# Four chained transformer blocks on one core: the second feed-forward product with its operands swapped

## The reference, cut to what matters

```
ca = _mha(x, enc_output, enc_output, memory_mask, ca_wq, ...)
x  = _ln(x + ca, ln2_g, ln2_b)
ff = relu(x @ ff_w1 + ff_b1) @ ff_w2 + ff_b2      # 128 -> 512 -> 128
x  = _ln(x + ff, ln3_g, ln3_b)
```

## Time and profile before

| | |
|---|---|
| median of 3 runs | 814.97 us (814.9 to 818.01) |
| the profiled execution's own time | 817.6 us |
| its span, first to last instruction | 815.8 us |
| mean granted clock of TensorE, as a share of full speed | 0.944 |
| TensorE busy | 87% |
| VectorE busy | 65% |
| ScalarE busy | 55% |
| GpSimd busy | 37% |

### The profile page before, as it was taken

How to read it: one execution, slowest core, us unless ns; L and a number is a source line. 1 busy time by engine, 2 the same in 40 slices (tenths; PEclk the granted TensorE clock), 3 DMA queues, 4 the chain that set the end, 5 groups by cost and what they waited for, 6 DMA issues and landing times.

```text
span 815.8 us, 26360 instructions
## 1 busy us (share of the span) xinstructions
PE 708.1 (87%) x9248; PEld 471.6 (58%) x9248; DVE 531.0 (65%) x1329; ACT 445.2 (55%) x1242; POOL 304.5 (37%) x497
## 2 busy tenths in 40 slices
PE   2999999999999999999977977777724789999996
PEld 1565666777766666666654755555522456666774
DVE  0698888888888877788872422222222566888784
ACT  1466666766667777777653232222202434676884
POOL 2244444566665333326666100000036663443110
PEclk9999999999999999999986999999975767999998
DMA  8333333223233111111100101111112110111110
GB/s 252 85 79 82 86 81 83 54 60 89 81 91 104 31 28 34 35 27 47 41 22 36 36 26 41 39 42 40 30 39 63 44 39 22 31 30 29 47 42 27
DMA packets 61085, 44.85 MB, mean 55 GB/s; under 512 B 18240, under 2 KB 55488, under 8 KB 59840
## 3 DMA queue, kind: packets, MB, share of 16 engines
q1 hardware_dynamic: 56592, 27.42, 12.0%
q10 hardware_dynamic: 2352, 12.00, 6.0%
q0 software_dynamic: 2048, 4.20, 1.6%
HBM read 22.68 MB, written 14.61 MB: 46 GB/s over the span
## 4 chain that ended last, share of the span: by engine, by line
PE 66%; issue 14%; POOL 7%; DVE 6%; ACT 3%; DMA 1%; ACTq 1%; SPq 0%; POOLq 0%; DVEq 0%
PE ps L560 10%; PE ps L602 9%; PE ps L784 5%; PE ps L722 4%; PE ps L793 4%; PE ps L578 4%; PE ps L655 3%; DVE hid_t L1264 3%; PE ps L730 3%; PE ps L643 3%; PE ps L677 3%; POOL k_by_j L485 2%; PE ps L802 2%; PE ps L587 2%; PE ps L750 2%
## 5 line engine op out<-in xcount | busy, mean ns | idle before, releaser
L1065 DVE TENSOR_REDUCE top<-ps 128x16 f32<-128x1024 f32 (+1 forms) x96 | 108.9, 1134 | 67.7 <-PE ps L560 66.9
L560 PE MATMUL ps<-k_by_j,q_t 32*64 32x256 f32 (+1 forms) x1536 | 126.7, 401 | 0.4 <-issue 0.2
L602 PE MATMUL ps<-cst,prob 128*128 128x128 f32 x704 | 122.3, 295 | 0.8 <-ACT prob L920 0.7
L477 POOL TENSOR_TENSOR rstd<-spread,half_neg 128x1 f32<-128x1 f32 x80 | 44.3, 553 | 207.5 <-DVE spread L1157 119.2
L485 POOL TENSOR_TENSOR k_by_j<-k_t,cst 128x512 f32<-128x512 f32 (+1 forms) x96 | 94.8, 988 | 71.9 <-ACT k_t L901 36.8
L602 PEld LDWEIGHTS ps<-cst,prob 128*128 128x128 f32 x704 | 78.5, 146 | 62.6 <-issue 59.2
L1080 DVE TENSOR_TENSOR prob<-ps,top 128x1024 f32<-128x1024 f32 (+1 forms) x96 | 108.8, 1134 | 0.7
L920 ACT ACTIVATE prob<-prob 128x1024 f32<-128x1024 f32 (+1 forms) x96 | 94.8, 987 | 20.3 <-DVE prob L1080 19.4
L1031 DVE RECIPROCAL inv<-ps 128x128 f32<-128x128 f32 x96 | 91.6, 954 | 11.7 <-PE ps L730 7.8
L518 POOL DMA_INDIRECT got<-expert_out,source x32 | 30.8, 963 | 158.8 <-DMA expert_out<-rows_out 150.2
L1264 DVE COPY hid_t<-ps 128x512 f32<-128x512 f32 x39 | 27.0, 691 | 95.0 <-PE ps L802 95.0
(11 more groups left out here) (160 smaller groups left out, 1287.9 us busy)
## 6 DMA issues: line engine op xcount, KB each, us to landing
sorted_rows<-zero_rows ACTq DMA_DIRECT2D x32, 272.0 KB, 2.7
stage_x<-x_t SPq DMA_DIRECT2D x80, 64.0 KB, 1.8
mow<-in_mow SPq DMA_DIRECT2D x18, 256.0 KB, 3.1
stage_kv<-in_ctx_t SPq DMA_DIRECT2D x64, 64.0 KB
stage_m<-in_m SPq DMA_DIRECT2D x80, 32.0 KB, 1.9
rows_in<-sorted_rows SPq DMA_DIRECT2D x39, 64.0 KB, 1.8
expert_out<-rows_out SPq DMA_DIRECT2D x39, 64.0 KB, 1.5
wat<-in_wat ACTq DMA_DIRECT2D x1, 1280.0 KB, 6.5
```

What stands on the lines that cost most here:

```text
L560: mm = pe.matmul(ps[S * b:S * b + S, 2 * p + bank, r * nj * S:(r + 1) * nj * S].rearrange("p (h k) -> p h k", k=S), q_t[rows_g, p, S * b:S ...
L602: mm = pe.transpose(ps[:, 2 * p + half, k * 128:(k + 1) * 128], prob[:, p, q * 128:(q + 1) * 128], ident)
L1065: dve.tensor_reduce(top[:, p, 0:nh].rearrange("p (b h) -> p b h", b=2), sc, AX.X, ALU.max).then_inc(top_d, 1)
```

## The change

The second product takes `hid_f` as its stationary operand and `ffw2` as the moving one. Its result has tokens in partitions, so VectorE adds `x_tok` to it straight from bank 7. The ScalarE copy (L854), the transpose (L675), the quarter `TURN` and the semaphores `f_o` and `f_turn` go. The bias, now one number per column, is added once, ahead of everything, to the row `b2` that ends up in `x_tok` of phase 1; `x_t`, which feeds the first product, takes its own `b2` from `vec` and stays as it was. The next pair's F waited for `f_o` and now waits for `f_y`, since VectorE is now the one that reads bank 7.

```diff
-ROWS = [..., "bo0", "bo1", "bo4"]
+ROWS = [..., "bo0", "bo1", "bo4", "ffb2"]
...
                 pr = follows(at, OFF_FY, FF)                 # TensorE
                     wait_own(pe, f_r, pr)
                     for c in range(HC):
-                        mm = pe.matmul(ps[:, B_F, 0:TOK], ffw2[:, 0, c, :], hid_f[:, pr.p, c, :], start=c == 0, stop=c == HC - 1)
+                        mm = pe.matmul(ps[:, B_F, 0:D], hid_f[:, pr.p, c, :], ffw2[:, 0, c, :], start=c == 0, stop=c == HC - 1)
                     mm.then_inc(f_acc, 1)
...
                     wait_pair(pe, norm_d, pr)
-                    if pr.phase == FF or pr.phase == FF + 1:
-                        done = follows(at, OFF_FN, FF)
-                        if done is not None:
-                            wait_own(pe, f_y, done)
...
-                    done = follows(at, OFF_FY, FF)
-                    if done is not None:
-                        wait_own(pe, f_o, done)
-                        pe.transpose(ps[:, B_OUT, TURN], sum_f[:, done.p, :], ident).then_inc(f_turn, 1)
-
                     pe.matmul(ps[:, B_OUT, OUT], heads_t[:, pr.p, :], wat[:, pr.phase, 3, :], start=True, stop=True)
...
-                    wait_own(pe, f_o, pr, 1)
+                    wait_own(pe, f_y, pr, 1)                  # ahead of F
                     wait_pair(pe, xt_e, pr)
...
-                pr = follows(at, OFF_FY, FF)                 # ScalarE
-                if pr is not None:
-                    wait_own(act, f_acc, pr)
-                    wait_own(act, f_turn, pr, 2)
-                    act.activation(sum_f[:, pr.p, :], ps[:, B_F, 0:TOK], ACT.Identity, bias=v("ffb2")).then_inc(f_o, 1)
...
+                dve.tensor_tensor(rows[:, ROW["b2"], :], rows[:, ROW["b2"], :], rows[:, ROW["ffb2"], :], ALU.add).then_inc(set_bias, 1)
...
-                    wait_own(dve, f_turn, pr)                # VectorE
+                    wait_own(dve, f_acc, pr)
                     wait_own(dve, f_nn, pr, 2)
                     wait_pair(dve, res_d, pr)
-                    dve.tensor_tensor(y_f[:, p, :], ps[:, B_OUT, TURN], x_tok[:, pr.i, :], ALU.add).then_inc(f_y, 1)
+                    dve.tensor_tensor(y_f[:, p, :], ps[:, B_F, 0:D], x_tok[:, pr.i, :], ALU.add).then_inc(f_y, 1)
```

More of the change, by code:

```diff
@@ L60 @@
 VECS = ["bq0", "bk0", "bq1", "bk1", "bq4", "bk4", "bv0", "bv1", "bv4",
-        "g1", "b1", "g2", "b2", "n1", "n2", "n3", "gL2", "bL2", "ffb2", "l3b1", "l3b2"] + \
+        "g1", "b1", "g2", "b2", "n1", "n2", "n3", "gL2", "bL2", "l3b1", "l3b2"] + \
        [f"ffb1_{c}" for c in range(HC)]
 VCOL = {name: n for n, name in enumerate(VECS)}
-ROWS = ["g1", "b1", "g2", "b2", "g3", "b3", "gL2", "bL2", "bo0", "bo1", "bo4"]
+ROWS = ["g1", "b1", "g2", "b2", "g3", "b3", "gL2", "bL2", "bo0", "bo1", "bo4", "ffb2"]
 ROW = {name: n for n, name in enumerate(ROWS)}
@@ L240, in build @@
         B_PROJ, B_HEADS, B_OUT, B_F = 4, 5, 6, 7
-        XT, FB, OUT, TURN = (slice(128 * n, 128 * n + 128) for n in range(4))
+        XT, FB, OUT = (slice(128 * n, 128 * n + 128) for n in range(3))
         B_SH, B_SY = (0, 1), (2, 3)
@@ L269, in build @@
         kj_d, rstd_d, gsc_d, res_d = (sem(k) for k in ("kj_d", "rstd_d", "gsc_d", "res_d"))
-        f_h, f_r, f_acc, f_o, f_turn, f_y, f_st, f_ag, f_sp, f_rs, f_nn, f_z, f_w, f_x, f_ms, f_rr, f_xn, f_back, f_xt = (
-            sem(f"f_{k}") for k in ("h", "r", "acc", "o", "turn", "y", "st", "ag", "sp", "rs", "nn", "z", "w", "x",
+        f_h, f_r, f_acc, f_y, f_st, f_ag, f_sp, f_rs, f_nn, f_z, f_w, f_x, f_ms, f_rr, f_xn, f_back, f_xt = (
+            sem(f"f_{k}") for k in ("h", "r", "acc", "y", "st", "ag", "sp", "rs", "nn", "z", "w", "x",
                                     "ms", "rr", "xn", "back", "xt"))
@@ L460, in slot @@
                         pool.wait_ge(loaded["rows"], 16)
-                        pool.wait_ge(set_bias, 3)
+                        pool.wait_ge(set_bias, 4)
                     wait_pair(pool, norm_d, pr)
@@ L1021, in residuals @@
                     .then_inc(set_bias, 1)
-                dve.wait_ge(set_bias, 3)
+                dve.wait_ge(set_bias, 4)
             def slot(at):
```

## The result

The changed kernel takes 855.74 us (median of 4 runs, 854.63 to 857.09), the kernel before in the same measurement 815.6 us (814.9 to 818.01). The ratio is 1.0487, with a 95% interval of 1.046 to 1.0515: 40 us slower. The predicted range (834 to 856) holds it by 0.3 us; the predicted 843 is 13 us short. The profiled execution took 857.09 us, with a span of 855.3. Three executions of two kernels of the experiments took far longer than the rest (2729, 3354 and 1020 us), and the ratios leave them out.

What follows compares the result with a forecast made beforehand. TensorE was taken to set the pace, VectorE close behind. F's waits over 15 slots (28.0 us), slot 38's -0.1 and the bias row's 0.3 summed to +28.2, so 815.0 + 28 = 843 us; range 834 to 856.

Steps and rivals of the forecast that it cites:

- F waits for `y_f` of its own slot: F on TensorE overwrites bank 7, so must wait for VectorE's late sum in the same slot; 15 slots, 28.0 us together.
- The size of the wait: Delay of F per slot: 1.77 us fixed, 2.11 in the loop, 1.97 first two, 1.27 last two; 28.0 us.
- so an earlier OUT does not help it: In fixed slots `y` on VectorE follows the subtraction by 0.03 us, so VectorE's side gets no earlier.
- The transpose: One transpose a slot leaves TensorE in 16 slots: 0.13 us each, 2.1 us taken alone, at most 4.8.
- The copy on ScalarE: L854, 0.37 us, 16 times, goes; ScalarE idles ahead of it and then waits for TensorE, so it gives nothing.
- The 0.3 us for the bias row: Adding the bias is one more 128x128 row on VectorE near 32 us, taken in full at 0.3 us.
- PV stays behind F: TensorE products run in program order, so PV can't fill the gap: term 1.77 us, else 0.74 and sum about +12.
- the clock column should stay at 1.00 in this stage: Sign of the main forecast: TensorE keeps its upper clock in the feed-forward stage; 837 to 849 us, chance 0.72.
- the clock falls too: Rival: gaps of 1.6 to 2.0 us in 15 slots cost TensorE its upper clock; +10 to +27 us, chance 0.18.
- absorbed: Rival: TensorE's 0.25 us wait and VectorE's 0.33 us idle vanish in the new rhythm; +19, 834 us, chance 0.06.
- not slower: Rival: `f_y` is there before TensorE reaches F, leaving the transposes' gain; -2 to -4.8, 810 to 813 us, chance 0.04.

Runs made afterwards that it cites:

- e5_wait_only: Kernel before with one edit: F waits for `y_f` (`f_y`) instead of `f_o`, copy and transpose kept; 855.54 us against 821.82, ratio 1.0414.
- e1_early: Changed kernel with VectorE's sum `y_f` moved ahead of the same slot's row maximum; 814.31 us, ratio 0.9959; over 12 runs 812.48 us, ratio 0.9966.
- e6_other_bank: Changed kernel with the second product's result in the transpose's old quarter of bank 6; 811.57 us, ratio 0.9931; over 12 runs 813.38 us, 0.9972.
- e2_ahead_of_y: Changed kernel with VectorE's sum `y_f` moved to just ahead of `y`, behind the subtraction; 824.91 us, ratio 1.0113 to the kernel before.
- e3_behind_y: Changed kernel with the sum `y_f` just behind `y`, ahead of `y`'s statistics; 830.33 us, ratio 1.018; once more on another chip, 834.19 us.

## Why the prediction was right, and where it was not

- **F waits for `y_f` of its own slot.** Right, and in the predicted place 15 times. `e5_wait_only` shows that this wait alone makes a loss of that size, `e1_early` and `e6_other_bank` that without it none is left.
- **The size of the wait.** The sum over the 15 slots was 28.0 us, and 26.2 were measured (with five fillers). The fixed slots were to grow by 1.77 and grew by 1.52, the last two by 1.27 and grew by 1.0 and 1.1, the first two by 1.97 and grew by 1.89; in the loop 2.11 was predicted, and 9.94 against about 7.8 us is 2.1. Two terms were off. From the end of `y_f` to F it took 0.05 us outside the loop, where 0.23 had been put in, while 0.11 of that came back later (5.50 us from F to the row maximum against 5.39); in the loop it took 0.14 to 0.24. And VectorE's side of the slot did get earlier: `y` came 2.41 us behind the row maximum, not 2.58. The prediction had said "so an earlier OUT does not help it", from the 0.03 us between the subtraction and `y`. But in the earlier trace rows OUT ends at 222.68 and `y` starts 0.04 behind it. `e5_wait_only`, which keeps the transpose, tells the two apart:

```profile
253.99 1.22 DVE L1065 TENSOR_REDUCE top<-ps 128x16 f32<-128x1024 f32 x1 [1.19 <-PE ps L560]
255.13 0.18 DVE L1072 TENSOR_SCALAR neg_m<-stage_m 128x64 bf16<-128x64 int32 x1
255.25 1.22 DVE L1080 TENSOR_TENSOR prob<-ps,top 128x1024 f32<-128x1024 f32 x1
...
256.14 0.39 PE L677 MATMUL ps<-wat,heads_t 128*128 128x128 f32 x2
256.56 0.29 DVE L1146 TENSOR_TENSOR y<-ps,x_tok 128x128 f32<-128x128 f32 x1
```

Here the subtraction is as early as in the changed kernel (1.26 behind the row maximum, the mask row having taken 0.18 us and not 0.27), and `y` still comes 2.57 behind it, right behind OUT. So it is the transpose that held `y` back in the fixed slots too, and its removal gives back what the prediction gave to the loop alone.

- **The transpose.** Predicted 0.13 us a slot, 2.1 in all, when taken alone; the two kernels without a wait gain 0.18 in a fixed slot (7.59 against 7.77) and 2.2 in all. The copy on ScalarE was predicted to give nothing, and no run takes it away by itself. The 0.3 us for the bias row can't be seen: the changed profile reached the stage 0.8 us earlier, not later.
- **PV stays behind F.** It did: L713 starts when F's eight passes are through, in every slot. With that the term was 1.77, without it 0.74, and 1.52 was measured. The rule of the Trainium skill (PSUM — Partial Sum Buffer, Engine vs sequencer instructions), matrix products in program order, agrees with this trace.
- **The step that failed is the clock.** The prediction gave 0.72 to the case that "the clock column should stay at 1.00 in this stage", and 0.18 to the rival "the clock falls too". The rival is what happened. Its price was +10 to +27, for three to eight spells of up to 3.4 us each; measured were 14.9 us in one execution, within it, and 8.7 in the other, below it, from six spells each, of about 1.5 us but for two of 4.3 in the first. The argument against it, that the gap stands between dense products, and that a stretch with 2.04 us busy of 4 had kept the clock, was not enough. The row that spoke for it, the fall behind L677's 1.15 us of idle, was the better guide. That the time lies in the range is owed to its reach into this rival, and by 0.3 us: the sum of the forecast covers some 26 of the 40 us.
- The section HAM oscillation — how this bites in real kernels of the Trainium skill's page TensorE: Matmul & The Clock Gate describes this pattern, a fall to the lower clock caused by a wait (there for a DMA) in each turn of a loop. Here it came in 6 of 15 turns in both executions that were profiled, and not in each turn.
- **The other rivals.** Nothing was absorbed beyond the 0.25 us above, and "not slower" needed the sum ahead of `y`. Just ahead of it was not enough (`e2_ahead_of_y`, +8.8 us); ahead of the row maximum was (`e1_early`).

Open: what decides in which slot a spell begins. The same program had six spells in each of two executions, in partly other slots, two of them long in one and none in the other; `e3_behind_y` had one spell in one execution and none in the other. And the 41.2 us over the 15 slots are 1.7 more than the 39.5 of the whole span: the changed profile reached the stage 0.8 us earlier, and took 0.9 less behind it.

## What to carry to other kernels

When an operand swap lets the consumer change engine, look up where that consumer stands in its engine's order, for the producer's next write of the bank now waits for it. Here one 0.29 us row, which ended 1.5 us after TensorE had come to F, cost 26 us, and moving the row or using a free quarter of another bank turned 5% slower into 0.3% faster. And price a new gap on TensorE twice: in a loop that had no gap it may also take the clock, which was a quarter to a third of the loss. And when two rows end almost together ahead of a third, as the subtraction and OUT did ahead of `y`, the trace alone doesn't say which of them it waits for.

## What was not expected of the hardware

- Five products that nobody reads, placed in the gap, made the kernel 14.6 us faster (842.28 against 856.84), by keeping the granted clock at 1.00; with two, one profile has one spell in place of six.
- Gaps ahead of F of 0.37 to 0.63 us left the clock at 1.00 in all 15 slots (`e2_ahead_of_y`). With 0.58 us in the fixed slots and 1.05 to 1.16 in the loop (`e3_behind_y`) it fell in none or one of the 15. In the changed kernel, with 0.92 and 1.00 in the last two and 1.43 to 2.09 us in the other 13, it fell in 6.
- The mask row on VectorE (128x64) took 0.18 us in most slots and up to 0.50 in others. Two slots of `e6_other_bank`, with the row of GpSimd beside it:

```profile
218.95 0.45 POOL L465 TENSOR_TENSOR scaled<-normed,rows 128x128 f32<-128x128 f32 x1
...
219.17 0.28 DVE L1060 TENSOR_SCALAR neg_m<-stage_m 128x64 bf16<-128x64 int32 x1
...
241.88 0.45 POOL L465 TENSOR_TENSOR scaled<-normed,rows 128x128 f32<-128x128 f32 x1
241.94 0.44 DVE L1060 TENSOR_SCALAR neg_m<-stage_m 128x64 bf16<-128x64 int32 x1
```

In both the mask row ends 0.05 us behind the end of a GpSimd row that had begun before it. So it is in all 39 mask rows of over 0.2 us, of 289, between 140 and 305 us of the fourteen traces; where GpSimd's row began behind the mask row, the mask row took 0.18 us. Behind 305 us, 25 long ones have no computing row of GpSimd beside them. No run varied this by itself.
